# Layer 0 of a fused two-layer cross-attention kernel: value products by tile ahead of the key products, feature splits in a row on GpSimd, one shifted step ahead of each run of value products

## What is computed

```
h  = concat([ctx, x], axis=1)              # 256 + 256 rows of 512 features
q  = x @ q_w + q_b                         # 256 rows, 16 heads of 32
kv = h @ kv_w + kv_b                       # keys and values of 512 rows
attn = softmax(q k^T / 32, with a mask on the ctx keys)
o  = (attn v) @ out_w + out_b + x
x1 = gelu(rmsnorm(o) @ mlp_w1 + b1) @ mlp_w2 + b2 + x
```

## Time and profile before

| | us |
|---|---|
| median of the runs (2 runs: 2436.51 and 2437.75) | 2437.13 |
| profiled execution, its own time | 2439.91 |
| its span, from the first to the last instruction | 2438.1 |
| around the span | 1.8 |

### The profile page before, as it was taken

How to read it: one execution, slowest core, us unless ns; L and a number is a source line. 1 busy time by engine, 2 the same in 40 slices (tenths; PEclk the granted TensorE clock), 3 DMA queues, 4 the chain that set the end, 5 groups by cost and what they waited for, 6 DMA issues and landing times.

```text
span 2438.1 us, 42636 instructions
## 1 busy us (share of the span) xinstructions
PE 2326.6 (95%) x14322; PEld 1863.8 (76%) x14322; DVE 1059.3 (43%) x1942; ACT 1434.1 (59%) x3378; POOL 420.1 (17%) x521
## 2 busy tenths in 40 slices
PE   7999999999999999989999999999999999999998
PEld 6776777777666677768888888888878888888886
DVE  6444445555444444453221221221246556565563
ACT  4766777666666776664222222222237787787876
POOL 4111222222222211130000000000221211212110
PEclk9999999999999999989999999999999999999998
DMA  6444333344434444333110110110244555555553
GB/s 187 106 114 101 95 97 96 99 113 113 113 96 113 96 113 113 86 102 139 52 52 0 52 52 0 52 52 0 87 123 123 133 140 150 130 146 141 135 131 83
DMA packets 141970, 239.11 MB, mean 98 GB/s; under 512 B 25393, under 2 KB 59601, under 8 KB 139873
## 3 DMA queue, kind: packets, MB, share of 16 engines
q1 hardware_dynamic: 140512, 238.05, 37.2%
q10 hardware_dynamic: 1408, 0.41, 0.1%
HBM read 86.28 MB, written 25.21 MB: 46 GB/s over the span
## 4 chain that ended last, share of the span: by engine, by line
PE 40%; SPq 10%; DMA 2%; issue 1%; ACT 1%; DVE 0%; DVEq 0%
SPq L531 9%; PE item_ps L66 5%; PE item_ps L68 5%; PE item_ps L67 5%; PE score_ps L67 5%; PE score_ps L66 5%; PE score_ps L68 5%; PE o_ps L66 3%; PE o_ps L68 3%; PE o_ps L67 3%; PE score_ps L1407 2%; DMA l_stack<-l_qk 1%; PE score_ps L1433 1%; SPq L599 1%; SPq L552 0%
## 5 line engine op out<-in xcount | busy, mean ns | idle before, releaser
L845 ACT ACTIVATE score_ps<-score_ps,l_neg_max 128x512 f32<-128x512 f32 (+1 forms) x1024 | 566.2, 556 | 210.7 <-DVE l_neg_max L1087 202.1
L1087 DVE TENSOR_REDUCE l_neg_max<-score_ps 128x1 f32<-128x512 f32 (+1 forms) x768 | 500.8, 685 | 151.7 <-PE score_ps L1407 149.1
L1868 ACT ACTIVATE mlp_hidden<-score_ps,b_col 128x512 f32<-128x512 f32 x128 | 88.2, 689 | 498.8 <-PE score_ps L68 453.8
L66 PE MATMUL item_ps<-feats_h,weights_l 128*128 128x256 f32 (+1 forms) x1024 | 329.6, 322 | 47.4 <-POOL feats_l L699 21.9
L1407 PE MATMUL score_ps<-l_stack 97*128 97x512 f32 (+1 forms) x1024 | 308.7, 360 | 23.4 <-DMA l_stack<-l_qk 9.4
L68 PE MATMUL item_ps<-feats_h,weights_h 128*128 128x256 f32 (+1 forms) x1024 | 318.6, 311 | 0.0
L67 PE MATMUL item_ps<-feats_l,weights_h 128*128 128x256 f32 (+1 forms) x1024 | 318.5, 311 | 0.0
L1916 DVE TENSOR_TENSOR mlp_hidden_l<-mlp_hidden,mlp_hidden_h 128x512 fp32r<-128x512 f32 x128 | 91.6, 715 | 514.8 <-ACT mlp_hidden_h L1870 514.7
L865 ACT ACTIVATE l_probs<-score_ps 128x1024 f32<-128x1024 f32 x272 | 264.9, 1021 | 59.8 <-PE score_ps L1433 59.5
L66 PEld LDWEIGHTS item_ps<-feats_h,weights_l 128*128 128x128 f32 x1024 | 194.6, 190 | 85.1 <-issue 33.0
L1433 PE MATMUL score_ps<-l_stack 99*128 99x256 f32 x1536 | 243.0, 293 | 10.5 <-ACT l_probs L865 4.6
(11 more groups left out here) (164 smaller groups left out, 4011.4 us busy)
## 6 DMA issues: line engine op xcount, KB each, us to landing
l_stack<-room SPq DMA_DIRECT2D x254, 192.0 KB, 3.1
l_stack<-l_qk SPq DMA_DIRECT2D x254, 128.0 KB
l_stack<-room SPq DMA_DIRECT2D x130, 128.0 KB, 2.9
l_tokens<-in_features SPq DMA_DIRECT2D x16, 1024.0 KB, 4.8
l_stack<-l_qk SPq DMA_DIRECT2D x254, 64.0 KB
l_stack<-room SPq DMA_DIRECT2D x130, 64.0 KB, 2.9
l_rows<-in_x SPq DMA_DIRECT2D x16, 512.0 KB, 4.1
norm_transposed<-norm_room SPq DMA_DIRECT2D x16, 512.0 KB, 4.8
```

Of the source, the lines that this page charges most:

```text
L66: pe.matmul(out, left_l, right_h, start=start, stop=False)
L845: m = act.activation(e, e, ACT.Exp, bias=neg_max[:, q, h:h + 1], accum_out=row_sum[:, q, h:h + 1])
L1087: dve.tensor_reduce(out, bank, AXIS_X, ALU.max, negate=True).then_inc(max_done, 1)
L1868: act.activation(hidden[:, m % HBUF, :], hidden_ps[:, m % 4, :], ACT.Gelu_apprx_tanh, bias=b1_col[:, m:m + 1])
```

## The change

Five edits, all in layer 0:

1. Value tiles are ordered by tile, ahead of all items: slot 0 ("share") has block 0 of tile 3 and block 1 of tiles 2 and 3; slots 1 and 2 ("v") the four blocks of tile 0 and of tile 1; slots 3 and 4 ("late") blocks 2 and 3 of tiles 2 and 3. `v_ahead` keeps block 0 of tile 2 alone, so nine matmuls move from the end of an iteration into the next first pass, which now has 10 slots with other numbers of steps. The release of block 0 and block 1 of the features moves to the first two products of slot 2.
2. DVE copies tile 0 in slot 2, tile 1 in slot 3, tiles 2 and 3 in slot 5 (item 0's).
3. POOL splits four blocks in a row; `row_scale` and `normalise_rows` follow them. `turn_norm` and `copy_norm` move to slot 8 (item 3's), and `turn_norm` now waits for ACT's copy of shift half 0; `turn_shift` of half 0 no longer waits for `copy_norm`, that of half 1 still does.
4. In the second pass shifted step 4 comes ahead of run 0, and likewise 4g+4 ahead of run g; ACT's exponentials are issued in the matching order, that of step 4(g+1) ahead of `o_high` g.
5. In the last batch 15 pieces, tile by tile, stand ahead of score steps, the first being tile 0's; DVE copies the tiles behind step 19.

```diff
-    SLOT = ([("values", f) for f in range(FB)] if first else [("share", 0)]) + [("item", k) for k in range(MIXED)]
+    SLOT = [("share", 0)] + ([("v", 0), ("v", 1), ("late", 2), ("late", 3)] if first else [])
+    SLOT += [("item", k) for k in range(MIXED)]
...
-    STEPS_AT_FIRST = [3, 3, 3, 3, 3, 3, 3, 3, 2] if first else [2, 2, 2, 2, 2, 2, 2, 2]
-    STEPS_IN_SLOT = [3, 3, 3, 3, 3, 4, 3, 3, 3] if first else [1, 1, 1, 1, 0, 3, 3, 2]
+    STEPS_AT_FIRST = [2, 3, 3, 2, 2, 3, 3, 3, 3, 2] if first else [2, 2, 2, 2, 2, 2, 2, 2]
+    STEPS_IN_SLOT = [3, 3, 3, 2, 2, 3, 3, 3, 3, 3] if first else [1, 1, 1, 1, 0, 3, 3, 2]
...
-    V_AHEAD = FB if first else 2
-    V_ORDER = [PLAIN_V, PLAIN_V + 1, 0, 1] if first else [0, 1]
+    V_AHEAD = 1 if first else 2
+    V_COPIES_IN_SLOT = {2: (0,), 3: (1,), AFTER_T: (2, 3)} if first else {}
     TURN_SLOT = AFTER_T + 1 if first else AFTER_T
-    NORM_SLOT = AFTER_T + 1
+    NORM_SLOT = AFTER_T + 3
...
-                    split_tokens(p, 0)
-                    split_tokens(p, 1)
+                    for f in range(FB):
+                        split_tokens(p, f)
                     if prev is not None:
                         row_scale(prev)
                         normalise_rows(prev)
-                    split_tokens(p, 2)
-                    split_tokens(p, 3)
...
                 exps(a, 3)
-                for g in range(FB - 1):
+                exps(a, KB)
+                for g in range(FB):
                     o_high(a, g)
-                    for s in range(KB * (g + 1), KB * (g + 2)):
+                    for s in range(KB * (g + 1) + 1, min(KB * (g + 2) + 1, PSTEPS)):
                         exps(a, s)
-                o_high(a, FB - 1)
...
-                    if k == AHEAD + 3 * FB:
+                    if k == SHIFT_MADE_AT:
                         for t in range(KB):
                             copy_v(a, t)
...
-                    if first and a is not None and slot == VALUE_SLOT:
-                        for t in range(KB):
+                    if a is not None:
+                        for t in V_COPIES_IN_SLOT.get(slot, ()):
                             copy_v(a, t)
...
+            def v_item(b, t, step):
+
+                at_least(pe, rows_done, QT * (b - 1) + t + 1)
+                pe.wait_ge(low_done, ITEMS * (b + 1) - 1 + t)
+                for f in range(FB):
                     step()
                     n = v_passes(b, t, f)
-                    if f == FB - 1:
-                        n.then_inc(v_done, 1)
-                if f < FB - 1:
-                    n.then_inc(v_shared, 1)
+                    if t == 1 and f < 2:
+                        n.then_inc(v_shared, 1)
+                n.then_inc(v_done, 1)
...
-                if first and norm_banks(a - 1) is o_ps:
+                if first and half == 1 and norm_banks(a - 1) is o_ps:
                     at_least(pe, nT_done, a)
...
                     values_copied(a + 2)
+                    pe.wait_ge(shift_copied, HALVES * (a + 1) + 1)
...
             def groups_of_four_keys(p, a, run, shifted):
+                shifted(a, KB)
                 run(0)
                 for g in range(1, FB):
-                    shifted(a, KB * g)
                     shifted(a, KB * g + 1)
+                    shifted(a, KB * g + 2)
                     if g == 1:
                         items_free(p)
                     project(a, g - 1)
-                    shifted(a, KB * g + 2)
                     shifted(a, KB * g + 3)
+                    if g < FB - 1:
+                        shifted(a, KB * g + 4)
                     run(g)
...
-                pieces = iter([(t, f) for f in range(FB) for t in V_ORDER[1:]])
+                pieces = iter([(t, f) for t in range(KB) for f in range(V_AHEAD if t == PLAIN_V else 0, FB)])
...
-                    if k < AHEAD + 3 * FB:
+                    if k < AHEAD + KB * FB - V_AHEAD:
                         next_of_v()
```

More of the change, by code:

```diff
@@ L887, in copy_v @@
             def copy_v(b, t):
-                act.wait_ge(v_done, KB * b + V_ORDER.index(t) + 1)
+                act.wait_ge(v_done, KB * b + t + 1)
                 at_least(act, pv_done, PSTEPS * b)
@@ L1138, in copy_v @@
             def copy_v(b, t):
-                dve.wait_ge(v_done, KB * b + V_ORDER.index(t) + 1)
+                dve.wait_ge(v_done, KB * b + t + 1)
                 at_least(dve, pv_done, PSTEPS * b)
@@ L1146, in last_first_pass_of_four_keys @@
                     step_max(a, k)
-                    if k == AHEAD + 3 * FB:
+                    if k == SHIFT_MADE_AT:
                         for t in range(KB):
                             copy_v(a, t)
-                    if k == SHIFT_MADE_AT:
                         make_shift(a, 0)
@@ L1370, in v_ahead @@
                 for f in range(V_AHEAD):
-                    n = v_passes(b, PLAIN_V, f)
-                if V_AHEAD == FB:
-                    n.then_inc(v_done, 1)
+                    v_passes(b, PLAIN_V, f)
             def v_share(b, f):
@@ L1380, in v_share @@
                 for t in range(PLAIN_V, KB):
-                    if f < V_AHEAD and t == PLAIN_V and not at_first:
+                    if f < V_AHEAD and t == PLAIN_V and (first or not at_first):
                         continue
@@ L1385, in v_share @@
                         n.then_inc(v_done, 1)
-                if f < FB - 1:
+                if f < FB - 1 and (not first or f == 2):
                     n.then_inc(v_shared, 1)
@@ L1517, in next_of_v @@
                         pe.wait_ge(o_low_done, FB * a)
-                    elif f == 0:
+                    elif f == 0 and t < PLAIN_V:
                         pe.wait_ge(rows_done, QT * (a - 1) + t + 1)
@@ L1573, in iteration @@
                         turn_norm(prev)
-                    if kind == "values":
-                        values(a, n, step)
+                    if kind == "v":
+                        v_item(a, n, step)
+                    elif kind == "late":
+                        v_share(a, n)
                     elif kind == "item":
```

## The result

The changed kernel takes 2375.47 us (two runs, 2373.96 and 2376.97) against 2437.13: a ratio of 0.9747, 95% interval 0.9705 to 0.9789, 61.7 us less. The forecast was 2384 with a range of 2367 to 2403. In the profiled executions the span fell from 2438.1 to 2372.1.

A forecast was written before the change was run, and what follows sets the result against it. PE was taken to bound the loop iteration. Per iteration -3.6 us, over 14 iterations -50.7, first iteration -0.4 and last batch -2 gave -53: 2437.1 to 2384 us, range 2367 to 2403 (forecast's own 2370 to 2394).

The forecast's parts named there:

- copies, splits and rows: First pass: PE's waits for value-tile copies (1.72 us), POOL's feature splits (1.33 and 0.12) and the previous batch's rows (0.29) go.
- step 8: First pass, slot 0: this score step would newly wait for the sum of step 4, +0.35 us an iteration with restart.
- step 18: First pass, slots 3 and 4: needs the sum of step 14; even within 0.2 us either way, booked at +0.15.
- the earlier tail: First pass's end: ACT and DVE about 0.6 us less behind, shrinking a PE wait; -0.25 us, bounds 0 and -0.49.
- without a gap: Second pass, expected sign: the 24 matmuls of run 0 would be followed by the other 8 with no wait.
- groups 1 to 3: Second pass: both orders were said to contain the same work without a wait on PE, so costed at nothing.
- The ends: Layer 0 outside the loop: first iteration -0.4 us, last batch -2 us with bounds -4 and +6.
- rival 1: First pass becomes bound by the chain of maxima and sums: 1.2 us more per iteration, 2401 us; chance 0.27.
- rival 2: First pass: POOL's row of splits is late at 3.35 us each, 4.3 us of wait, 2445 us; chance 0.04.
- rival 3: Clock stays low longer at the last batch or falls elsewhere: about 8 to 10 us more, 2393 us; chance 0.07.
- rival 4: First pass's tail paid back: `copy_norm` delays DVE before the last maxima, gain about 2.3 us per iteration, 2403 us; chance 0.05.
- The rule on shared SBUF interfaces: First pass: value copies moved beside POOL's splits would not disturb them, their source being PSUM; a split takes 2.09 us.

The follow-up runs named there:

- run 0: Not a follow-up run: the second pass's first run of 32 weigh matmuls on PE; in the kernel before, 24 of them took 2.15 us, 0.51 lost.
- half-stack run: Own semaphore for the mask and first eight of sixteen DMAs refilling stack half 0, layer 0: changed kernel 2351.1 us; same edit on the kernel before 2430.8 us.

## Why the prediction was right, point by point

- **PE bounds the iteration, and its waits are what can be won.** Right. The period fell by 4.24 us with the same matmuls, and the two entries of the earlier trace rows are gone.
- **The first pass.** Forecast -3.2 us (copies, splits and rows -3.46, step 8 and step 18 +0.50, the earlier tail -0.25), measured -3.82 with that half alone. Copies, splits and rows went as walked; item 0 at T+14.1, the last split's end at T+16.3 for T+16.2. Step 8 cost 0.49 where 0.35 was booked; step 18 cost nothing: no wait for a sum is left in the loop but step 8's. The undersized term is small restarts, which I had left out. At 595.4 and 595.6, 602.1, 605.1 and 605.5, and 607.3 of the old trace, PE's starts are 0.07 to 0.10 over the pitch, 0.5 us an iteration; in the new trace they are not there. I take them for places where ACT and DVE were barely in time, but no bracket names an engine. The third block was also read too low: ahead of its restart, from 586.55 to 586.90, stand another 0.12 us. That makes -3.46 - 0.12 - 0.51 + 0.49 = -3.6 of the -3.82; the last 0.2 I can't place. The booked -0.25 was for another one, the wait ahead of shifted step 2, and that stayed: 0.33 idle before, 0.29 after.
- **The second pass.** Forecast -0.41, measured -0.42 on top of the first half and -0.46 alone. What lies ahead of shifted step 7 came as walked: shifted step 4 fills 0.48 us of the gap ahead of weigh 3, and project 0 starts 0.02 later (614.10 to 615.38 before, 577.46 to 578.76 now) where 0.10 was booked. The gap itself was larger than read, 2.15 - 24 x 0.058 = 0.75, which is why 0.17 us of idle time is left in each iteration and the sign "without a gap" failed. What lies behind shifted step 7 was wrong: costing groups 1 to 3 at nothing was the step that failed. The earlier trace rows had it: 32 weigh matmuls in 2.19 us. I read 0.068 as the pitch; it is 1.87 / 32 = 0.058, and the last eight of each run had waited for their exponential. At that pitch the first 24 of the run at 617.89 are over at 619.29, and the exponential that the last eight read ended at 619.46:

```profile
617.52 1.94 ACT L865 ACTIVATE l_probs<-score_ps 128x1024 f32<-128x1024 f32 x2 [0.70 <-PE score_ps L1433]
```

Too short a wait to empty the pipeline, it has no bracket. So edit 4 frees 3 x 0.32 there, and the other sentence of the same paragraph, that PE has the same instructions between shifted step 7 and the next score step, was right of the instructions and wrong of the time: they became 0.96 us shorter, the refill did not, and its wait grew by 0.87. Two omissions of nearly one size cancelled, and that the total of this pass still came out is luck to that extent. By the half-stack runs, 1.54 against 0.42, they were worth 1.1 us an iteration.
- **The ends.** Forecast -2.4; layer 0 outside the loop gave -4.3. The 2.9 ahead of the loop are not shown to be the change's. With the new first pass alone the loop begins at 103.43, against 103.54 before and 100.69 with the whole change. And the half-stack run and the one with the last copies spread, which issue the same there, begin it at 99.57 and 101.44, as the clock between 60 and 70 us was at 1.00 or at 0.72. In the last batch the first value product did wait for DVE's rows (0.78 idle), and the clock's low stretches there sum to 13.7 us where the kernel before had 20.5. A wait of 3.3 us for the shift, behind the four copies, was not in the forecast.
- **The rivals.** A bound by maxima and sums (rival 1) is refuted by their one small wait. POOL late (rival 2) did not happen, with 0.4 us to spare, but the run with the row work between the splits shows what it would cost: the price of 4.3 for the wait was a third short, mostly since the clock falls with it. So at such a split that rival would have ended further on the slow side than the 2445 us given, which is argued and not measured. The clock (rival 3) and the tail (rival 4) did not come.
- **The rule on shared SBUF interfaces.** Splits with a value copy beside them (551.65 to 552.96, with DVE's copies from PSUM at 552.30) are as long as the others, 2.09. The Trainium skill (GPSIMD Engine Reference, section Key points) names DVE operations in a 2-port mode or with two SBUF inputs; these copies have one input, from PSUM. So far trace and rule agree again; no row shows the mode of a copy.

## What to carry to other kernels

Price a wait by distances between starts, not by the idle time the profile brackets, and take the pitch from a stretch that can't be waiting; a pitch that two kernels disagree on is a wait. When a gain lies between two ends of a transfer's chain, ask which end the transfer starts from: only what is won ahead of its start is won at its end. And a semaphore that counts a whole group of transfers makes the first reader wait for the last: one more for the part that is read first was worth 24 us here once PE had become fast enough to notice.

## What the runs showed of the hardware that was not expected

How the same idle time is cut matters to TensorE's clock. In the kernel before, PE waited 1.46 us, worked 3.0 and waited 1.06, in every iteration, at the full 2.4 GHz level (PEclk 1.00 in the earlier trace rows). One wait of 2.99 us was followed by the 1.2 GHz level in every iteration of the loop, though in one of them only behind the second wait, and one of 2.2 us in nine of fourteen. With that, waits worth about 4.6 us at the full clock cost 6.6. Three waits for the stack, of 1.66 to 1.88 us, were followed by it too, where none of the changed kernel's in the loop, up to 1.89, was. So the length of a wait alone doesn't decide it, and no run here shows what does. The Trainium skill (TensorE: Matmul & The Clock Gate, section Part 1: The HAM clock gate) has the array's clock follow how busy the engine was of late; the runs agree, and they show a fall behind a single wait of 2.2 us with work on either side of it.
